# Moving the turns of the values behind each weight transposition, one step sooner, and planning the head loads around them

## The reference

```python
q = (x @ Wq + bq).reshape(1, B * N, H, hd)            # 16 heads of 32
kv = (cond @ Wkv + bkv).reshape(1, -1, 2, H, hd)
...
q, k = _fq_sym(q, axis=-1), _fq_sym(k, axis=-1)       # one step per row
v = _fq_sym(v, axis=2)                                # one step per channel, over all 5776 rows
attn = softmax(einsum('bhqd,bhkd->bhqk', q, k))
attn = _fq_unsigned(attn, axis=-1)                    # 0 to 255, one step per query row
out = einsum('bhqk,bhkd->bhqd', attn, v) @ Wp + bp
...
x = x + attention(layernorm(x), ctx); x = x + ffn(layernorm(x))
```

## Time and profile before

| | |
|---|---|
| median of 3 runs | 1847.7 us (1845.15 to 1850.2) |
| profiled execution | 1847.68 us, its span 1845.9 us |
| granted TensorE clock, mean | 0.982 |
| DVE busy | 1691.0 us, 92% of the span |
| PE busy | 1631.2 us, 88% |
| ACT, POOL busy | 1391.7 us (75%), 1375.3 us (75%) |
| DVE's share of the chain that ended last | 57% |

### The profile page before, as it was taken

How to read it: one execution, slowest core, us unless ns; L and a number is a source line. 1 busy time by engine, 2 the same in 40 slices (tenths; PEclk the granted TensorE clock), 3 DMA queues, 4 the chain that set the end, 5 groups by cost and what they waited for, 6 DMA issues and landing times.

```text
span 1845.9 us, 41823 instructions
## 1 busy us (share of the span) xinstructions
PE 1631.2 (88%) x17032; PEld 1153.6 (62%) x17032; DVE 1691.0 (92%) x2670; ACT 1391.7 (75%) x1362; POOL 1375.3 (75%) x759
## 2 busy tenths in 40 slices
PE   7997899989888888888898898888889888789998
PEld 6884666666566666655566666555555555478876
DVE  6869999999999999999999999999999999986665
ACT  2446898888988898889888988897888888742232
POOL 1432789898879888888898889887898798753232
PEclk9999999999999999999999999999999999989999
DMA  5578988998899899989998998889888998732221
GB/s 175 193 224 201 209 187 177 184 196 166 181 186 198 176 193 184 187 164 177 191 200 177 181 196 170 158 158 181 168 169 157 205 185 160 166 116 45 67 58 47
DMA packets 851530, 309.96 MB, mean 168 GB/s; under 512 B 784966, under 2 KB 813964, under 8 KB 851212
## 3 DMA queue, kind: packets, MB, share of 16 engines
q1 hardware_dynamic: 851340, 307.29, 81.0%
HBM read 74.26 MB, written 39.59 MB: 62 GB/s over the span
## 4 chain that ended last, share of the span: by engine, by line
DVE 57%; PE 21%; issue 9%; POOL 7%; DMA 5%; ACT 1%; SPq 1%; POOLq 0%; DVEq 0%; ACTq 0%
DVE S L1295 51%; PE PS L876 5%; POOL PT L1529 5%; PE PK L913 3%; DMA PP<-Pr 3%; PE PS L743 2%; PE PK L682 2%; PE PK L684 2%; PE PS L711 2%; DVE MJ L1321 1%; PE PO L684 1%; DVE kam L1186 1%; PE PO L682 1%; DVE VMX L1190 1%; PE PO L762 1%
## 5 line engine op out<-in xcount | busy, mean ns | idle before, releaser
L1295 DVE TENSOR_SCALAR_CACHE_REDUCE S<-PS,SQN 128x1536 f32<-128x1536 f32 (+1 forms) x768 | 1283.2, 1714 | 20.5 <-PE PS L743 10.1
L1529 POOL CAST PT<-PP 128x3072 uint16<-128x3072 uint8 (+1 forms) x400 | 1048.5, 2650 | 223.6 <-DMA PP<-Pr 217.7
L1088 ACT ACTIVATE Pr<-S,MS 128x5888 uint8<-128x5888 f32 x200 | 1041.2, 5206 | 166.7 <-DVE MJ L1321 140.0
L743 PE MATMUL PS<-KT,QT 96*128 96x512 bf16 (+1 forms) x2496 | 633.4, 373 | 153.2 <-DVE S L1295 140.0
L762 PEld LDWEIGHTS PO<-VI,PT 128*128 128x128 f16 x9200 | 338.4, 96 | 199.6 <-issue 31.3
L743 PEld LDWEIGHTS PS<-KT,QT 96*128 96x128 bf16 (+1 forms) x2496 | 191.5, 99 | 364.9 <-DVE S L1295 131.1
L762 PE MATMUL PO<-VI,PT 128*128 128x32 bf16 x9200 | 356.3, 178 | 20.1 <-ACT AO L1038 9.7
L684 PE MATMUL PK<-CT,WG 128*128 128x128 f32 (+1 forms) x1288 | 212.7, 293 | 7.0 <-DMA CT<-ctxt 7.0
L682 PE MATMUL PK<-WG,CT 128*128 128x128 f32 (+1 forms) x1288 | 210.7, 293 | 6.3 <-ACT VF L949 3.7
L684 PEld LDWEIGHTS PK<-CT,WG 128*128 128x128 f32 x1288 | 169.1, 194 | 10.0 <-issue 7.8
L682 PEld LDWEIGHTS PK<-WG,CT 128*128 128x128 f32 (+1 forms) x1288 | 167.0, 192 | 8.5 <-issue 6.6
(11 more groups left out here) (156 smaller groups left out, 1538.0 us busy)
## 6 DMA issues: line engine op xcount, KB each, us to landing
CT<-ctxt SPq DMA_DIRECT2D x180, 256.0 KB, 3.2
k_rows<-KS SPq DMA_DIRECT2D x39, 512.0 KB, 4.0
q_rows<-QS SPq DMA_DIRECT2D x13, 512.0 KB, 4.6
W13F<-w13T SPq DMA_DIRECT2D x12, 352.0 KB, 3.7
PP<-Pr SPq DMA_TRANSPOSE x200, 6.0
XT<-x SPq DMA_DIRECT2D x12, 256.0 KB, 4.4
XR<-x SPq DMA_DIRECT2D x12, 256.0 KB, 3.3
base_rows<-XO SPq DMA_DIRECT2D x12, 256.0 KB, 3.3
```

The source lines that it names most:

```text
L743: last = pe.matmul(PS[n % 2][p0:p0 + r, f:f + w], QT[h % 3][0:PARTS * HD, q0:q0 + r], KT[h % 3][0:PARTS * HD, c * CHUNK + f:c * CHUNK + f ...
L1088: act.activation(Pr[i % 2].rearrange("p t q b -> p t b q"), S[i % 2].rearrange("p (t b q) -> p t b q", b=2, q=P), ACT.Exp, bias=MS[:, i % ...
L1295: v.tensor_scalar(S[i % 2][:, c * CHUNK:c * CHUNK + CW[c]], PS[n % 2][:, 0:CW[c]], neg_step, None, ALU.mult, ALU.min, accum_out=MN[:, i % ...
L1529: gp.tensor_copy(PT[i % 2][:, 2 * t0:2 * t1, :].rearrange("p (t b) q -> p t b q", b=2), PP[i % 2][:, t0:t1, :].bitcast(U8).rearrange("p t ...
```

## The change

Three things change. The turns of the values move, in SP's order, from ahead of PP(i) to behind it, and their steps, those of `v_round` and those of POOL's casts are set by a table `V_AT`, counted from E + 3 and not E + 4; `v_step` moves from step E + 4 to E + 3. POOL's casts are due just ahead of a step's widening and no longer between its halves. And the plan of transfers counts a turn as twice the load, in its new place, and counts the four loads of WP.

```diff
+V_STEP = 3
+V_AT = (0, 1, 2, 2, 3, 4, 4, 5, 6, 6, 7, 7)
...
-            load[STEP_OF_UNIT[g, NU - 1] + 5 + b * 2 // 3] += P
+            load[STEP_OF_UNIT[g, NU - 1] + V_STEP + 3 + V_AT[b]] += 2 * P
+    for k in range(NK):
+        load[WP_AT + k] += P * C // 256
...
-        v_step_of = {STEP_OF_UNIT[g, NU - 1] + 4: g for g in range(1, NG)}
+        v_step_of = {STEP_OF_UNIT[g, NU - 1] + V_STEP: g for g in range(1, NG)}
...
-                v_rounds.setdefault(STEP_OF_UNIT[g, NU - 1] + 4 + b * 2 // 3, []).append((g, b))
+                v_rounds.setdefault(STEP_OF_UNIT[g, NU - 1] + V_STEP + V_AT[b], []).append((g, b))
...
-                v_turns.setdefault(STEP_OF_UNIT[g, NU - 1] + 6 + b * 2 // 3, []).append((g, b))
+                v_turns.setdefault(STEP_OF_UNIT[g, NU - 1] + V_STEP + 2 + V_AT[b], []).append((g, b))
...
-                for g, b in v_turns.get(i, []):
-                    turn_v(g, b)
                 if i >= 2:
                     sp.wait_ge(M["s_un"], NCAST * (i - 1))
                 sp.dma_start_transpose(PP[i % 2], Pr[i % 2].rearrange("p t q b -> p (t q b)").bitcast(U16)).then_inc(s_tr[i % 2], 16)
+                for g, b in v_turns.get(i, []):
+                    turn_v(g, b)
...
                 T = VS3[:, g % 2]
+                chain.sync()
...
-                             (end + 5.95 + b * 2 / 3, v_quant, (g, b))]
+                             (end + V_STEP + 1.95 + V_AT[b] + 0.01 * b, v_quant, (g, b))]
```

## The result

| | before | changed |
|---|---|---|
| median of 7 runs each, on one chip | 1847.7 us (1845.1 to 1850.2) | 1855.5 us (1852.2 to 1860.3) |
| ratio | | 1.0039, 95% interval [1.0027, 1.0051] |
| profiled execution, its span | 1847.68, 1845.9 us | 1860.31, 1858.5 us |
| granted TensorE clock, mean | 0.982 | 0.976 |

The forecast was 1845.9 us with a range of 1838 to 1855; the time lies 0.5 us above the range and 7.8 us above before. The profiled execution of the changed kernel was the slowest of its seven. From the MJ row of step 4 to that of step 199 it took 1411.5 us (201.80 to 1613.33), before 1405.2 (198.12 to 1603.30): 6.3 us are lost inside the steps, which is most of the 7.8 between the medians. The rest of the span's 12.6 us lies ahead of the steps (3.7) and behind them (2.6), where the change touches nothing.

What follows compares the result with a forecast made beforehand. DVE, busy 92% of the span, was taken as the bound. A gain of 14.8 us less 7.5 (ring), 1.8 (PE's slowness), 3.6 (tail) and `v_step` made -1.8: 1845.9 us, range 1838 to 1855.

Steps and rivals of the forecast that it cites:

- gain in 54, 104, 152 to 156: DVE stalls behind late PP vanish, as head pieces and turns no longer stand ahead of it on SP: 14.8 us saved.
- ring: POOL's cast of batch b waits until turn b - 3, now behind PP, has landed: 7.5 us in sum.
- Step 49: Turn 6 lands late, delaying cast, rounding and the exponential of step 49 by 2.4 us: 1.0 us lost in step 51.
- PE's slowness: PE computes scores more slowly after a wait: 0.6 us a group added, 1.8 in all.
- Step 52: Batch 11's cast waits for turn 8, delaying PT(48) and PE's scores in step 52: 0.95, 0.95 and 2.3 us.
- tail: SP's backlog after late PP(50) delays the exponentials of steps 55 and 57: 1.2 us a group, 3.6 in all.
- DVE's slack: Around step 49, DVE needs an exponential 6.8 us after MJ and it ends 5.4 after: 1.4 us of lateness costs nothing.
- Slower: SP's backlog persists; exponentials of steps 55 and 57 stall DVE 2 us each in groups 1 and 2: 1856 us, chance 0.22.
- The third rival: Only the head-piece plan matters; PP(50) stays late by POOL, group 3 gains 3: 1844.7 us, sharing the forecast's 0.52.
- the fast rival: The ring fits into the slack, only group 3 pays, 9 to 14 us saved: 1837 us, chance 0.26.

Runs made afterwards that it cites:

- five buffers: The changed kernel with five buffers for the cast values instead of three, two of them in a tile free at that time: 1840.3 us, ratio 0.9950 to before.
- the copies first: The changed kernel with ACT's copies of the next step's unit moved ahead of the rounding of the values: 1855.1 us, ratio 1.0033 to before.
- the plan alone: The kernel before with only the head pieces at the changed kernel's steps; turns, casts and rounding as before: 1837.65 us, ratio 0.9938.

## Why the prediction was wrong, by its own steps

| term of the sum | forecast | changed kernel, by step |
|---|---|---|
| gain in 54, 104, 152 to 156 | -14.8 | -3.9, -3.1, -7.2: -14.2 |
| ring: lateness of "Step 49" | 1.0 in each group (+0.6 for PE's slowness) | 4.3, 2.5, 3.7 |
| ring: "Step 52" | 0.95, 0.95, 2.3, and 0.1 each for the exponential of step 52 | 2.0, 0.6, 3.6 |
| tail in 55, 57 | 1.2 in each group | 2.4, 1.7, 0 |
| `v_step` | 0.1 | 0.13 three times |
| sum | -1.8 | +7.0 |

For 152 to 156 the measured spacing is 37.68, of which 3.59 are the new stall in 152 (10.39 less a plain 6.80), so that 34.09 are left of 41.32. This split is a choice: before, step 152 took 8.63, and with five buffers 8.70, so up to 1.9 of the 3.6 us need not be the ring's. The sum is 0.7 above the 6.3 us by the first and the last MJ; other steps differ by so much.

**The step that failed is "Step 49"**, the price of the wait at the ring in the first stall of each group. The root of its mechanism was right (a turn lands late, a cast, the rounding, the exponential), its size was not: 10.5 us, where the sum had 3.0 and the 1.8 for PE's slowness. That is 5.7 of the 8.8 us between the two sums. "Step 52" was 1.7 too low, the tail 0.5, the gain 0.6 too high, and `v_step` 0.3 too low. The lateness of the exponential, forecast as 2.4 us, was 4.0. Three things were missing.
- *Where SP stood.* I let PP(47) go out as its exponential ended and added 1.3 us for a key piece. It went out 2.4 us late: with a turn behind a PP of 4.4 us SP had no gap left before the key piece. I took the landing of a turn as 3.0 us; the median is better (2.4), but turn 5 took 4.3. In group 3 it came a batch earlier: turn 4 took 4.3 as well, and the cast of batch 7 waited 3.26 us for it.
- *Who else waits for ACT.* I held the exponential's lateness against DVE's slack of 1.4 us. By that rule the 4.0 us it was late (532.71 against 528.75) would have given 2.6, in step 51. I had put the unit's copies into ACT's time, but not asked who waits for them: PE's projection, with the scores of step 50 behind it, a step sooner and with no such slack. The kernel with the copies first shows what this is worth: it tells where the lateness was paid, and not how much, for with that way closed steps 49 to 51 lost the same. In group 3 there are no units, and there the rule holds: the exponential of step 148 was 3.3 us late, and DVE waited 1.85 in step 150, on which PE's late scores (1.02 and 0.63 more) come. ACT and DVE after:

```profile
1257.16 0.72 ACT L936 ACTIVATE VQ<-VV,VS 128x512 int8<-128x512 f32 x1 [3.47 <-POOL VB L1481]
1257.79 5.19 ACT L1092 ACTIVATE Pr<-S,MS 128x5888 uint8<-128x5888 f32 x1
...
1263.11 1.82 DVE L1300 TENSOR_SCALAR_CACHE_REDUCE S<-PS,SQN 128x1536 f32<-128x1536 f32 x1 [1.85 <-ACT Pr L1092]
```

- *PE after a wait.* 0.6 us a group was half of what one stall of before had cost on top of its wait. In step 50, with a granted clock of 0.80, the loss was 0.9 us above PE's wait of 2.8.

"Step 52" was right in mechanism, and its idle of 7.83 us ahead of the cast of batch 11 was above the 5 to 7 expected, since its turn 8 started from an exponential that was already late. In groups 2 and 3 that idle was 5.29 and 4.75 us. In group 3 the price was too low by 1.3. The ring is not all that is late there: with five buffers step 52 took 8.88 us, by way of PP's landing.

The rival that the time fell to was *Slower* by its size (1856), but not by its mechanism: the tail in steps 55 and 57 was 4.1 us in all and not 2 in each of four steps. That its time was met is luck. The third rival, that only the plan matters, was half right in a way in which I had not put it: the plan is the whole gain (-12 us alone, not -3), and the turns' move is all loss (0.5% by itself, 1.0% on top of the plan). The time of some 2 us for PP, estimated from the Trainium skill (Advanced Engine Details and Errata, X-Bar Transpose), which had kept the fast rival's chance up, was not seen: PP took 5.6 to 7.3 us to land between 500 and 590 of the changed kernel.

Open: which of the moved head pieces carries the gain in each group (the plan also moved the queries of heads 6 and 10 from steps 54 and 104 to 59 and 109, and the later pieces of head 14 from 164, 167, 170 to 167, 170, 172, which the list ahead of the prediction leaves out); and why stretches that nothing touches (a 0.7 us in step 74, 90 or 124, 2 us in step 179) differ between kernels.

## What to carry to other kernels

Before a producer's hand-over is moved later in a queue, write the ring down batch by batch: how many steps lie between the release of a buffer and its next use, for the last batch too. Moving one entry by a step (the last batch, whose turn stood one step and not two behind that of the batch three before it) gave back three quarters of what five buffers gave here, and it can be seen in the table itself. When an engine is found to be late, list everything behind the waiting instruction on it and who waits for each. The first of them in time tells where the stall appears; closing that way alone gave nothing here, since the next one then paid. And when a change has two parts, time each alone: here one was worth 0.6% and the other cost 1.0%, and the one worth having is a table of load steps and no instruction.

## What the runs showed of the hardware that was not expected

- Waits of GpSimd that add up to 19 or 23 us (in 15 and 16 pieces) cost 0.3% against the plan alone; 43 us in 21 pieces 1.0%, 51.5 in 19 pieces 1.5%. Over these four the cost grows faster than the sum of the waits. Below them it tells nothing: 4.2 us of waits came with 0.1%, 7.7 with 0.2%, and these kernels differ in more than the waits.
- Turns issued behind PP land sooner after their own issue than those ahead of it (median 2.4 against 3.2 us; with the plan alone 3.0 ahead and 2.4 behind), so a landing measured from issue says little on how late the data are.
- The issue of a DMA transposition is no constant: PP took SP 3.5 to 4.7 us in one stretch of the changed kernel, and 5.1 at 1263.85, when two turns stood ahead of it.
